# Attention on one core: two groups of heads share one value-product bank, and one turn with 72 identity columns

## The reference

```python
def body(carry, kv):
    out, m, l = carry
    K_blk, V_blk = kv
    scores = jnp.einsum('bhqd,bhkd->bhqk', Q, K_blk) * SCALE
    M_ij = scores.max(axis=-1, keepdims=True)
    m_new = jnp.maximum(m, M_ij)
    corr = jnp.exp(m - m_new)
    exp_scores = jnp.exp(scores - m_new)
    chunk_sum = exp_scores.sum(axis=-1, keepdims=True)
    l_new = chunk_sum * corr + chunk_sum
    out_new = out * corr + jnp.einsum('bhqk,bhkd->bhqd', exp_scores, V_blk)
    return ((out_new, m_new, l_new), None)
```

## Time and profile before

| what | value |
|---|---|
| time, median of 3 runs | 1705.54 us (1704.27 to 1707.38) |
| the profiled execution's own time | 1710.11 us |
| its span, first to last instruction | 1708.3 us |
| mean granted TensorE clock over the span | 0.953 |
| PE busy over the span | 1545.1 us (90%) |
| DVE, ACT, POOL busy over the span | 1289.3, 1163.9, 714.1 us |
| value products L600, first and last start | 65.5 and 851.9 us |

### The profile page before, as it was taken

The page is one execution under the profiler, slowest core; times in us unless marked ns, Lnnn a source line. Parts: engine busy times, 40 slices in busy tenths (PEclk is TensorE's granted clock), DMA queues, the critical chain, the costliest instruction groups (busy, mean ns, idle before and its releaser), DMA issues. The chain is left out here.

```text
span 1708.3 us, 34433 instructions
## 1 busy us (share of the span) xinstructions
PE 1545.1 (90%) x8456; PEld 848.4 (50%) x8456; DVE 1289.3 (75%) x3545; ACT 1163.9 (68%) x2434; POOL 714.1 (42%) x1011
## 2 busy tenths in 40 slices
PE   3999999999999999999949999999989997996995
PEld 1333333333333333333337777777755655554774
DVE  4899999999999999999744766776757884323664
ACT  1488888888888888888826676666644545563663
POOL 2224334344433434433341333333334442474887
PEclk7699999999999999999959999999999997998998
DMA  5222333232233323241000000000030000444442
GB/s 121 59 86 83 89 88 94 74 90 85 78 90 88 93 75 89 73 144 56 10 7 1 1 1 0 0 0 0 13 91 1 1 1 11 143 153 126 141 136 67
DMA packets 83649, 109.24 MB, mean 64 GB/s; under 512 B 15947, under 2 KB 48977, under 8 KB 83552
## 3 DMA queue, kind: packets, MB, share of 16 engines
q1 hardware_dynamic: 77152, 91.28, 18.9%
q0 software_dynamic: 6400, 16.82, 2.8%
HBM read 63.24 MB, written 40.08 MB: 60 GB/s over the span
## 5 line engine op out<-in xcount | busy, mean ns | idle before, releaser
L841 DVE TENSOR_REDUCE bmax<-PS 128x8 f32<-128x512 f32 x1024 | 650.9, 682 | 60.2 <-PE PS L579 57.8
L691 ACT ACTIVATE EX<-PS 128x512 f32<-128x512 f32 x1024 | 564.1, 603 | 102.6 <-PE PS L590 93.4
L579 PE MATMUL PS<-KR,QR 33*128 33x512 f32 x1024 | 408.5, 468 | 38.6 <-DVE bmax L841 24.9
L590 PE MATMUL PS<-QR,KR 64*128 64x512 f32 x1024 | 396.3, 459 | 1.6 <-ACT EX L691 1.5
L579 PEld LDWEIGHTS PS<-KR,QR 33*128 33x128 f32 x1024 | 166.2, 188 | 351.5 <-DVE bmax L841 296.1
L600 PE MATMUL PS<-EX,VS 128*9 128x512 f32 x2048 | 268.6, 596 | 1.2 <-ACT EX L691 1.2
L590 PEld LDWEIGHTS PS<-QR,KR 64*128 64x128 f32 x1024 | 161.5, 185 | 11.2 <-ACT EX L691 10.2
L1026 PE MATMUL PS<-pA,wb 128*128 128x512 f32 x640 | 155.9, 401 | 0.0
L776 POOL TENSOR_TENSOR m_diff<-m_prev,m_all 128x16 f32<-128x16 f32 x64 | 14.3, 223 | 311.2 <-DVE m_all L853 311.2
L1026 PEld LDWEIGHTS PS<-pA,wb 128*128 128x128 f32 x640 | 121.3, 193 | 25.6
L1179 ACT ACTIVATE gelud<-PS,scales 128x512 f32<-128x512 f32 x128 | 88.3, 690 | 57.3 <-PE PS L1026 57.3
(11 more groups left out here) (230 smaller groups left out, 2781.9 us busy)
## 6 DMA issues: line engine op xcount, KB each, us to landing
QR<-q_scr SPq DMA_DIRECT2D x256, 64.0 KB, 2.4
KR<-k_scr SPq DMA_DIRECT2D x256, 64.0 KB, 2.3
big<-row_scr SPq DMA_DIRECT2D x72, 192.5 KB, 2.4
k_scr<-partsB SPq DMA_DIRECT2D x42, 256.0 KB, 2.9
q_scr<-partsB SPq DMA_DIRECT2D x28, 256.0 KB, 2.9
X<-in_L_attn_x SPq DMA_DIRECT2D x16, 256.0 KB, 2.9
X<-x SPq DMA_DIRECT2D x16, 256.0 KB, 2.5
xB<-in_L_attn_x SPq DMA_DIRECT2D x14, 256.0 KB, 3.1
```

The source lines that it names most:

```text
L579: pe.matmul(PS[:, bank_of(i, n), :], QR[rows, i, h // 2, t * P:(t + 1) * P], KR[rows, i, h // 2, :], start=True, stop=True).then_inc(tile_ ...
L590: pe.matmul(PS[:, RING3 + bank_of(j, n), :], KR[rows, j, h // 2, kt * P:(kt + 1) * P], QR[rows, j, h // 2, :], start=True, stop=True).then ...
L691: act.activation(EX[:, n % (2 * HG), :], PS[:, RING3 + bank_of(j, n), :], ACT.Exp, scale=SCALE).then_inc(ex_set, 1)
L841: dve.tensor_reduce(bmax[:, i % 2, n, :], PS[:, bank_of(i, n), :].rearrange("p (b k) -> p b k", k=BLK), AX_X, ALU.max).then_inc(tile_max, 1)
```

## The change

The groups of a chunk are taken in pairs, an even and an odd one. `VS` has 18 columns a head: an even group's values and sum column stand in columns 0 to 8, an odd one's in 9 to 17, and the others are zero. The value products of both groups accumulate in bank 6 without a restart between them, so that rows 32h to 32h+17 hold both. `copy_out` and `outputs` then run once a pair, in even steps; the turn is four plain matmuls with `OT` as the stationary and 72 chosen columns of the identity (18 of each 32) as the moving operand, and `take` copies 288 columns in place of 512. `den` and `rden` are made once a pair with 32 columns, in odd steps, and `AOs` by two instructions, one for each group. `PER_CHUNK` and the counts of the waits follow. The core of the diff:

```diff
-        VS = sb("VS", [P, NG, NT, HG, HD + 1], F32, att)
+        VS = sb("VS", [P, NG, NT, HG, 2 * (HD + 1)], F32, att)
...
-                dve.memset(VS[BLK:P, :, NT - 1, :, HD], 1.0).then_inc(vs_preset, 1)
+                for a in range(2):
+                    dve.memset(VS[BLK:P, a:NG:2, NT - 1, :, a * (HD + 1) + HD], 1.0).then_inc(vs_preset, 1)
...
-                return "outputs" if 0 <= g - 3 < GROUPS else None
+                return "outputs" if i % 2 == 0 and 0 <= g - 3 < GROUPS else None
...
-                    if kt == 0 and some(g):
-                        pe.wait_ge(ot_set, g)
+                    if kt == 0 and j % 2 == 0 and some(g):
+                        pe.wait_ge(ot_set, pair(c, j))
                     for h in range(HG):
-                        mm = pe.matmul(PS[32 * h:32 * h + HD + 1, 6, :], VS[:, j, kt, h, :],
-                                       EX[:, kt % 2 * HG + head_T(h), :], start=(kt == 0), stop=(kt == NT - 1))
+                        mm = pe.matmul(PS[32 * h:32 * h + 2 * (HD + 1), 6, :], VS[:, j, kt, h, :],
+                                       EX[:, kt % 2 * HG + head_T(h), :], start=(j % 2 == 0 and kt == 0),
+                                       stop=(j % 2 == 1 and kt == NT - 1))
...
-                        turn(OT)
+                        used = idf[:].rearrange("p (h d) -> p h d", d=32)[:, :, 0:2 * (HD + 1)]
+                        for t in range(NT):
+                            mm = pe.matmul(PS[:, 7, t * COLS:(t + 1) * COLS].rearrange("p (h d) -> p h d", h=HG),
+                                           OT[:, t * P:(t + 1) * P], used, start=True, stop=True)
+                        mm.then_inc(use_done, 1)
...
-                        act.copy(OTT[:], bank).then_inc(use_read, 1)
+                        act.copy(OTT[:].rearrange("p t x -> p (t x)"), PS[:, 7, 0:NT * COLS]).then_inc(use_read, 1)
...
-                        if n == 1 and has(3):
+                        if n == 1 and has(3) and i % 2 == 0:
                             copy_out(g - 3)
...
-                            if has(4):
+                            if has(4) and i % 2 == 1:
                                 denominators(b, i, g)
...
-                            if has(4):
-                                normalise(b, i, g)
+                            if has(4) and i % 2 == 1:
+                                normalise(b, i)
```

More of the change, by code:

```diff
@@ L364, in block_kernel @@
         corr = sb("corr", [P, NG, NT * HG], F32, p2)
-        den = sb("den", [P, NT * HG], F32, p2)
-        rden = sb("rden", [P, NT * HG], F32, p2)
+        den = sb("den", [P, NT * HG, 2], F32, p2)
+        rden = sb("rden", [P, NT * HG, 2], F32, p2)
         xnB = sb("xnB", [P, S], F32, p2)
@@ L433, in block_kernel @@
         uses = [(b, i, q) for b in range(NCH + 2) for i in range(NG) for q in range(NT) if kind_of(b, i, q)]
-        PER_CHUNK = 4 * NG - 1
         STEADY = 3
+        PER_CHUNK = sum(1 for b, _, _ in uses if b == STEADY)
         ENDING = NCH - 2
@@ L467, in some, with pair @@
             return not (isinstance(n, int) and n <= 0)
+        def pair(b, j):
+            return b * (NG // 2) + j // 2
         TG = NT * HG
@@ L729, in take @@
                     elif k == "outputs":
-                        if some(g - 3):
-                            act.wait_ge(nrm_steps, (g - 3) * 3)
-                        act.copy(OTT[:], bank).then_inc(use_read, 1)
+                        if some(g - 4):
+                            act.wait_ge(nrm_steps, pair(*behind(b, i, 3)) * N_STEPS)
+                        act.copy(OTT[:].rearrange("p t x -> p (t x)"), PS[:, 7, 0:NT * COLS]).then_inc(use_read, 1)
                     elif k == "rows":
@@ L751, in step @@
                         if n == 8 and has(1):
-                            correction((i - 1) % NG, g - 1)
+                            correction(*behind(b, i, 1), g - 1)
                 run_groups(act, step, TAIL + 1)
@@ L862, in denominators, with inverses, normalise @@
+                    dve.scalar_tensor_tensor(den[:], corr[:, j - 1:j + 1, :].rearrange("p a k -> p k a"), 1.0, sums,
                                              ALU.add, ALU.mult).then_inc(nrm_steps, 1)
-                def inverses(g):
-                    dve.wait_ge(nrm_steps, (g - NG) * 3 + 1)
+                def inverses(b, i):
+                    dve.wait_ge(nrm_steps, pair(*behind(b, i, NG)) * N_STEPS + 1)
                     dve.reciprocal(rden[:], den[:]).then_inc(nrm_steps, 1)
-                def normalise(b, i, g):
-                    dve.wait_ge(nrm_steps, (g - NG) * 3 + 2)
-                    if i == 0 and some(b - 1):
+                def normalise(b, i):
+                    c, j = behind(b, i, NG)
+                    dve.wait_ge(nrm_steps, pair(c, j) * N_STEPS + 2)
+                    if j == 1 and some(b - 1):
@@ L871, in normalise @@
                         dve.wait_ge(use_done, use(b - 1, NG - 1, 3) + 1)
[L872 to L877 removed]
+                    o = OTT[:].rearrange("p t (h a d) -> p t h a d", a=2, d=HD + 1)
@@ new lines, in normalise @@
+                    r = rden[:].rearrange("p (t h) a -> p t h a", t=NT)
+                    for a in range(2):
+                        dst = AOs[:].rearrange("p (t x) -> p t x", t=NT)[:, :, (j - 1 + a) * HG * HD:(j + a) * HG * HD]
+                        dve.tensor_tensor(dst.rearrange("p t (h d) -> p t h d", d=HD), o[:, :, :, a, 0:HD],
+                                          r[:, :, :, a].unsqueeze(3).broadcast_to([P, NT, HG, HD]),
+                                          ALU.mult).then_inc(nrm_steps, 1)
```

38 lines of the change are left out of this document (17 added, 21 removed).

## The result

The changed kernel is slower: 1717.76 us (median of 4 runs, 1715.52 to 1719.03) against 1705.08 us (median of 4, 1704.27 to 1707.38), a ratio of 1.0071 with a 95% interval of 1.0053 to 1.0088. That is +12.7 us where +3 was forecast, and it lies outside the range of 1699 to 1715. The profiled execution took 1717.67 us (span 1715.9).

What follows compares the result with a forecast made beforehand. PE and VectorE were taken to hand the path to each other, neither bounding all. Terms of +0.23 us a chunk gave +3.3 over 14.5 chunks; with +0.7 for loads and -0.9 correction, about +3: 1708.5 us, range 1699 to 1715.

Steps and rivals of the forecast that it cites:

- The turn in even steps: PE's turn in i = 0 and 2: 1.04 us as plain matmuls for 0.58, +0.46 on the path each.
- The first rival: Moving columns pace the turn: 0.70 us, about 1699.5; by the page's figure 0.50, about 1694; chance 0.12.
- VectorE's part: VectorE's normalising: even steps save 0.15 (i = 0) and 0.24 (i = 2); larger odd-step work costs +0.10 a chunk.
- The odd steps: i = 1 and 3 without their turn: -0.20 us each, second `AOs` paid; larger `den` and `rden` +0.10 a chunk.
- the cover of the second `AOs`: Odd steps: VectorE's next wait of 0.35 us covers the second `AOs`' 0.15 and leaves 0.20.
- The hold of the product: Odd steps: quarter 3's value product waits for quarter 2's exponentials, starting 1.7 us after the tiles; gain 0.22.
- The wider loads: Value products' stationary operands of 18 columns for 9: +2 ns a load, 0.7 us in all, at most 2.
- the fourth rival: Wider loads make each value product 0.03 us longer: 5 us more, 1713; chance 0.08.
- The correction: -0.9 us, between 0 and 2, for places where ScalarE's relief or a shared wait returns a little.
- The third rival: PE bounds nearly everywhere, so VectorE's 0.39 returns nothing and odd gains are lost: +0.92 a chunk, 1719 us; chance 0.12.
- new wait for ScalarE: Odd steps: PE's value product waits 0.36 us for ScalarE; the third rival has it help lose the odd steps' 0.20.
- its test: The third rival decides once PE no longer shows its waits for VectorE, 0.32 and 0.34 before, in even steps.

Runs made afterwards that it cites:

- e8: Kernel before without `den`, `rden` and `AOs` in even steps (those groups not normalised): ratio 0.9997 to the kernel before.
- e7: Kernel before without the turn of `OT` in odd steps, all copies kept: ratio 0.9969 to the kernel before.
- e12: Kernel before without odd-step turns and even-step normalising, with odd steps' `den` and `rden` on 32 columns and `AOs` written twice: ratio 0.9979.
- e9: Kernel before with a second `AOs` product, into an unused buffer, in odd steps: ratio 0.9995 to the kernel before.
- e10: e5 with the value product of quarter 3 in odd steps issued one score tile later: ratio 0.9972 to the kernel before.
- e3: Kernel before with 18 columns in each stationary operand of the value products, 9 of them unused: ratio 1.0015.
- e1: Changed kernel with four transpositions in place of the plain matmuls of the turn: 1704.14 us beside 1705.36 of the kernel before.
- e5: Changed kernel with the turn by transpositions and the first pair's `rden` and `AOs` moved from i = 1 to i = 2: 1701.18 us beside 1707.61 before.
- e2: Kernel before with all four turns of `OT` as plain matmuls of 128 columns: 1737.37 us, ratio 1.0192.

## Why the prediction was wrong

**The turn in even steps was right** in size, 1.04 us, and in its eight instructions for four matmuls. That the loads pace them fits, as 56 columns fewer of 128 saved only 0.05 us; no run changed the loads to show it. By the isolated gap in the Trainium skill, TensorE: Matmul & The Clock Gate, section Back-to-back issue gap, the passes of 72 columns would be 33 ns apart and the turn near 0.50; the section itself says that this formula counts too little at small widths, and the trace does not agree with it. The first rival falls.

**The step that failed is VectorE's part**, one half in the even steps and one in the odd ones. For the even steps the prediction has: "In i = 0 only `rden` is on the path (VectorE has it up to 440.09): -0.15. In i = 2 `den` and `rden` are: -0.24". i = 0 came nearly as forecast, -0.12, and PE's wait went from 0.32 to 0.22. i = 2 returned 0.00 of its 0.24. The prediction says that VectorE has the path in quarters 0 and 1 of i = 2 and names no wait of PE that `den` and `rden` would shorten. The trace of before has none. Its one wait of PE for VectorE in i = 2 is missing from the earlier trace rows though it is the longest of a chunk, and it stands at the step's first tile, ahead of `den` (412.92):

```profile
408.80 0.50 PE L579 MATMUL PS<-KR,QR 33*128 33x512 f32 x1 [0.55 <-DVE bmax L841]
```

It is 0.55 in e8 and in the changed kernel too. A row of operations without a gap shows that an engine is full, not that it is the bound. With the work taken out (e8), gaps appear as waits for PE, and the ten reductions take 7.10 for 7.00 us.

**The odd steps** were forecast at -0.40 for the missing turns, with the second `AOs` paid, and +0.10 for the rest, -0.30 together. Measured are -0.37 + 0.29 = -0.08. The turns' own return, 0.37 (e7), is a little under the 0.44 that I had set before the charge. The larger `den` and `rden` cost 0.13 in i = 1 (e12), near the 0.10. What failed is the cover of the second `AOs`: "VectorE's next wait of 0.35 covers 0.15 of extra normalising". That wait is still there in the changed kernel, 0.29 at 411.83, but it comes behind the fourth score tile of quarter 3. PE reaches that tile early now and waits for a bank that VectorE has to free, so what VectorE does before it is passed on, and the idle time behind it covers nothing. With the turn in place PE came later and the second `AOs` was free (e9). No run has the second `AOs` alone without the turn, so its price by itself, about 0.16 a chunk (0.29 less 0.13), is an estimate from these runs.

**The hold of the product** I put on the exponentials of quarter 2, which would release it 1.70 us after the tiles. In the changed kernel it is 1.81, behind a fourth tile that waits for its bank. e10 starts the product 0.6 us later still and loses nothing, so its start did not set the time there. A product ahead of the waiting tile was not run.

**The wider loads** cost more than the 0.7 us in the sum (e3, +1.0 to +4.1 us), less than the 5 of the fourth rival. **The correction** of -0.9 us for relief of ScalarE had no row under it, and e1 beside e12 shows no such relief.

**The third rival** gave +0.92 a chunk and 1719 us, with a chance of 0.12, and came nearest. Its reason holds in part: VectorE's saving returned 0.12 of 0.39, and the odd steps' gain was lost to the doubled work. Its new wait for ScalarE is not what the runs show, and its test fails. PE's waits of the earlier trace rows are still there after, 0.45 in i = 1 and, in i = 0,

```profile
444.14 0.50 PE L586 MATMUL PS<-KR,QR 33*128 33x512 f32 x1 [0.21 <-DVE bmax L854]
```

So its number came near with half of its mechanism, and partly by luck.

What stays open: the measured parts leave 0.04 a chunk, the second `AOs` has no run of its own without the turn, and no run moves the product ahead of the waiting tile.

## What to carry to other kernels

When two engines hand the path to each other, ask at each place which of them has a wait that the other ends; an engine that runs without a gap but lets no one wait gives nothing back when it is relieved. An idle stretch covers added work only if no other engine waits for this one between the work and the stretch; check that this still holds in the changed order. And before merging passes to halve a turn, look whether the merged form is still a transposition: here pairing was a gain of 0.32% with transpositions and the first pair's normalising moved to i = 2 (e5), and a loss of 0.71% with plain matmuls.

## What the runs showed of the hardware

- A plain fp32 matmul of 128 rows and 72 columns is hardly shorter in a row than one of 128: eight instructions take 1.04 us to the next tile against 1.09, and their loads are the full 191 ns each. The turn by transpositions takes 0.58. This held wherever it was put: 0.50 us a turn in e2, 0.46 in e1.
- Loads of 18 columns last 96 ns, more than the 94 of 32 columns in the earlier trace rows, where I had interpolated 90 from 88 and 94. So load time does not go by columns alone here.
- A reciprocal on 32 columns lasts 342 to 343 ns, on 16 columns 243: 99 ns for 16 more. `den` grew from 177 to 207, twice the 15 ns I took from the slope of `AOs`.
- Two `AOs` in a row take 0.48 us where one takes 0.28: the second displaces 0.20, more than the 0.15 that one displaces between reductions.
